# Node rows split into two parts of 12 bits in place of three of 8 for the gathering products of a graph kernel

## What is computed

```python
src, dst = (edge_index[0], edge_index[1])
for i in range(L):                      # L = 3
    msg = jax.nn.relu(x[src] + edge_attr)
    aggr = jax.ops.segment_sum(msg, dst, num_segments=N_NODES)
    h = x + aggr
    h = h @ W1[i] + b1[i]
    h = jax.nn.relu(_bn(h, g_mlp[i], be_mlp[i]))
    h = h @ W2[i] + b2[i]
    h = _bn(h, g_out[i], be_out[i])
    if i != L - 1:
        h = jax.nn.relu(h)
    x = h
```

## Time and profile before

| | us |
|---|---|
| median of 3 runs | 4912.82 (4910.23 to 4918.35) |
| profiled execution | 4920.59 |
| its span, first to last instruction | 4918.9 |
| busy in the span: TensorE / VectorE / GpSimd / ScalarE | 4251.6 / 3977.6 / 3219.8 / 2696.7 |

### The profile page before, as it was taken

How to read it: one execution, slowest core, us unless ns; L and a number is a source line. 1 busy time by engine, 2 the same in 40 slices (tenths; PEclk the granted TensorE clock), 3 DMA queues, 4 the chain that set the end, 5 groups by cost and what they waited for, 6 DMA issues and landing times.

```text
span 4918.9 us, 143637 instructions
## 1 busy us (share of the span) xinstructions
PE 4251.6 (86%) x50439; PEld 4136.7 (84%) x50440; DVE 3977.6 (81%) x7711; ACT 2696.7 (55%) x6908; POOL 3219.8 (65%) x2584
## 2 busy tenths in 40 slices
PE   2556655489999999969999997999999979999998
PEld 2556555489999999969999996999999969999996
DVE  7788888167777777778888887988888878888887
ACT  3899999257777777753343334433433353333334
POOL 0088888327777777737777773677777637777773
PEclk7777777699999999989999998999999989999998
DMA  9955554757777778758888885788888848888884
GB/s 123 319 188 193 171 190 166 240 161 250 248 249 249 248 249 249 239 177 278 278 281 282 279 279 170 245 279 281 279 276 281 271 145 281 277 279 282 277 280 135
DMA packets 664981, 1183.55 MB, mean 241 GB/s; under 512 B 152090, under 2 KB 489836, under 8 KB 664828
## 3 DMA queue, kind: packets, MB, share of 16 engines
q1 hardware_dynamic: 440796, 833.33, 53.3%
q10 hardware_dynamic: 142848, 181.89, 12.2%
q0 software_dynamic: 81184, 166.43, 10.3%
HBM read 966.87 MB, written 214.44 MB: 240 GB/s over the span
## 4 chain that ended last, share of the span: by engine, by line
PE 78%; issue 9%; DVE 6%; SPq 2%; DMA 1%; DVEq 1%; ACTq 1%; ACT 1%; POOL 0%; POOLq 0%; PEld 0%; PEldq 0%
PE ps L1721 24%; PE ps L1707 15%; PE ps L1636 13%; PE ps L1623 10%; PE ps L1731 6%; PE ps L1585 3%; PE ps L1586 3%; PE ps L1575 3%; DVEq L1420 1%; PE ps L1775 1%; DVE src_turned L1400 1%; DVE dst_hot L1407 1%; ACTq L823 1%; DVE agg L1422 1%; DVE sums L1415 0%
## 5 line engine op out<-in xcount | busy, mean ns | idle before, releaser
L728 POOL DMA_INDIRECT unit_x<-gin_rows,unit_src x1449 | 1788.3, 1234 | 670.3 <-PE ps L1721 389.5
L680 POOL DMA_INDIRECT attr_by_slot<-abuf,ridx x1080 | 1372.6, 1271 | 539.7 <-issue 328.0
L1721 PE MATMUL ps<-dst_hot,sums 128*128 128x128 f32 x10584 | 1520.7, 284 | 79.2 <-DVE agg L1422 71.4
L937 ACT ACTIVATE sums<-sums 128x512 f32<-128x512 f32 x1512 | 823.6, 571 | 1285.5 <-DVE sums L1415 1263.4
L1721 PEld LDWEIGHTS ps<-dst_hot,sums 128*128 128x128 f32 x10584 | 1306.9, 193 | 98.0 <-DVE agg L1422 84.4
L1707 PE MATMUL ps<-x_parts,src_turned 128*128 128x128 bf16 x15876 | 1143.5, 220 | 36.3 <-POOL x_parts L714 32.0
L1707 PEld LDWEIGHTS ps<-x_parts,src_turned 128*128 128x128 bf16 x15876 | 1027.0, 99 | 55.5 <-issue 40.3
L1415 DVE TENSOR_TENSOR sums<-ps,sums 128x512 f32<-128x512 f32 x1512 | 895.9, 615 | 8.4 <-PE ps L1707 8.4
L1407 DVE TENSOR_TENSOR dst_hot<-iota_one,dl_slot 128x896 f32<-128x896 f32 x756 | 818.9, 1083 | 2.2 <-DVE agg L1460 2.2
L846 ACT ACTIVATE val<-ps,val 128x128 f32<-128x128 f32 x2597 | 718.0, 375 | 180.5 <-DVE val L1261 180.5
L1636 PE MATMUL ps<-val,src_hot 128*128 128x129 f32 x5194 | 697.7, 284 | 1.9 <-DVE sums L1201 1.2
(11 more groups left out here) (242 smaller groups left out, 4133.4 us busy)
## 6 DMA issues: line engine op xcount, KB each, us to landing
sums<-attr_by_slot SPq DMA_DIRECT2D x756, 448.0 KB, 3.6
src_turned<-rows_by_group SPq DMA_DIRECT2D x756, 224.0 KB
turned_hot<-rows_by_block ACTq DMA_DIRECT2D x392, 384.0 KB
attr_by_slot<-zeros SPq DMA_DIRECT2D x36, 3136.0 KB, 17.1
unit_attr<-in_edge_attr SPq DMA_DIRECT2D x204, 448.0 KB
abuf<-in_edge_attr SPq DMA_DIRECT2D x72, 960.0 KB
unit_x<-gin_rows,unit_src POOLq DMA_INDIRECT x1449
attr_by_slot<-abuf,ridx POOLq DMA_INDIRECT x1080
```

Of the source, the lines that this page charges most:

```text
L680: pool.indirect_dma_start(out=attr_table, out_offset=bass.IndirectOffsetOnAxis(ap=ridx[:, g, t0 + t:t0 + t + 1], axis=0), in_=abuf[:, k % ...
L728: pool.indirect_dma_start(out=unit_x[:, half_place(k), t, :], out_offset=None, in_=gin_rows[n], in_offset=bass.IndirectOffsetOnAxis(ap=uni ...
L937: act.activation(attr[:, first:first + tiles, :], attr[:, first:first + tiles, :], ACT.Relu).then_inc(s_msg, 1)
L1721: ins = pe.matmul(ps[:, 7, 0:WINDOW], attr[:, b, :], dst_hot[:, HOT[c], b % G_TILES, :], start=(b == 0), stop=(b == BLOCKS - 1))
```

## The change

- The three bf16 parts become two of type float32r, a four-byte form of which a part holds 12 bits: `x_high`, ScalarE's copy of the rows to that type, and `x_low`, VectorE's difference. `x_high` lies over `flat`.
- Each tile has two products in place of three, and the ones (`src_turned`) become float32r too, in four buffers by HOT; SyncE loads the lanes to `src_rows` (bf16), behind a wait for the turning in place of the gather. VectorE's turning waits for the gather that last read the buffer.
- The parts are made at the end of a layer: VectorE copies turned chunks to `x_stage` (seven stages), SyncE stores them from there, two in flight, ScalarE makes the high part behind its normalising, VectorE the low part one chunk later. GpSimd has no part in it. In the first layer the rows lie in `work` (the tile of the attributes), and SyncE's first loads wait until they are turned, split and stored.
- KEEP_AT goes from 0 to 2: a unit's window addition comes at h = 9 and h = 2. TURN_LEAD stays 3 by value.

```diff
--- before.py
+++ after.py
...
+STAGES = 7
 G_LEAD = 3
 FIRST = 4
-TURN_LEAD = 3
+TURN_LEAD = min(HOT_SINCE)
 ADD_AT = 3
 SUM_AT = 4
-KEEP_AT = 0
+KEEP_AT = 2
...
-LAST_LEFT = BY_UNIT + 1
+LAST_LEFT = BY_UNIT + KEEP_AT + 1
...
-        x_parts, end = placed("x_parts", [P, PARTS, BLOCKS, D], BF16, at)
+
+        x_high, end = placed("x_high", [P, BLOCKS, D], F32R, at - 4 * COLS)
+        x_low, end = placed("x_low", [P, BLOCKS, D], F32R, at)
         dst_hot, at = placed("dst_hot", [P, HOTS, G_TILES, P], F32, end)
-        src_turned, at = placed("src_turned", [P, BLOCKS * P], BF16, at)
+        src_rows, at = placed("src_rows", [P, BLOCKS * P], BF16, at)
+        src_turned, at = placed("src_turned", [P, HOTS, G_TILES * P], F32R, at)
+
+        x_stage, _ = placed("x_stage", [P, STAGES, CHUNK], F32, at)
...
+        gx, gy = (of_moments[:, k * D:(k + STEP) * D].rearrange("p (s d) -> p s d", d=D) for k in range(2))
+        ghot = of_stat[:, 0:STEP * P].rearrange("p (s d) -> p s d", d=P)
...
-        s_gin_row = sem("gin_rows_stored")
+        s_gin_row = [sem(f"gin_rows_stored{k}") for k in range(2)]
...
+        def rows_stored(n, c):
+
+            return 16 * (n * len(range(c % 2, CHUNKS, 2)) + c // 2 + 1)
+
+        def all_stored(eng, n):
+            for c in (CHUNKS - 2, CHUNKS - 1):
+                eng.wait_ge(s_gin_row[c % 2], rows_stored(n, c))
...
+            def store_rows(n, of, ready):
+
                 for c in range(CHUNKS):
                     ready(c)
-                    rows = to[c * CHUNK:min((c + 1) * CHUNK, NODES)]
-                    sp.dma_start(rows if c == CHUNKS - 1 else rows.rearrange("(b p) d -> p b d", p=P),
-                                 rows_of(flat, c)).then_inc(done, 16)
+                    if c >= 2:
+                        sp.wait_ge(s_gin_row[c % 2], rows_stored(n, c - 2))
+                    rows = gin_rows[n][c * CHUNK:min((c + 1) * CHUNK, NODES)]
+                    sp.dma_start(rows if c == CHUNKS - 1 else rows.rearrange("(b p) d -> p b d", p=P), of(c)).then_inc(s_gin_row[c % 2], 16)
...
-                sp.wait_ge(s_gath, G_HALVES * done + 2 * c + 2 - G_HALVES + G_HALVES)
-                sp.dma_start(src_turned[:, c * G_TILES * P:(c + 1) * G_TILES * P],
+                if not isinstance(g, int) or done > 0:
+                    sp.wait_ge(s_sturned, G_CHUNKS * done + c + 1 - G_CHUNKS)
+                sp.dma_start(src_rows[:, c * G_TILES * P:(c + 1) * G_TILES * P],
...
-            sp.wait_ge(s_var, 2)
+
+            sp.wait_ge(s_turned, TURNS["gin_in"] + CHUNKS)
+            sp.wait_ge(s_low, CHUNKS)
+            all_stored(sp, 0)
             load_group(0, 0)
...
+                if n > 0:
+
+                    sp.wait_ge(s_low, CHUNKS * (n + 1))
+                    all_stored(sp, n)
...
-                for c in range(G_CHUNKS):
-
-                    of = slice(c * G_TILES, (c + 1) * G_TILES)
-                    pool.wait_ge(s_part, 2 * (G_CHUNKS * n + c) + 2)
-                    pool.tensor_tensor(x_parts[:, 2, of, :], unit_x[:, c % 2, :, :], x_parts[:, 1, of, :], ALU.subtract).then_inc(s_last, 1)
-                pool.wait_ge(s_last, G_CHUNKS * (n + 1))
-                pool.wait_ge(s_gin_row, 16 * CHUNKS * (n + 1))
+                pool.wait_ge(s_low, CHUNKS * (n + 1))
+                all_stored(pool, n)
...
+                if n == 0:
+                    for c in range(CHUNKS):
+                        normed(act, c)
+                        of = slice(BY_CHUNK * c, min(BY_CHUNK * (c + 1), BLOCKS))
+                        act.activation(x_high[:, of, :], work.rearrange("p (b d) -> p b d", d=D)[:, of, :], ACT.Copy).then_inc(s_high, 1)
+                        keep_columns(c)
...
+                def high_part(c):
+
+                    act.wait_ge(s_copied, TURNS[f"gin_out{n}"] + c + 1)
+                    if c == CHUNKS - 1:
+                        act.activation(x_high[:, BLOCKS - 1, :], x_stage[:, c % STAGES, 0:D], ACT.Copy).then_inc(s_high, 1)
+                    else:
+                        act.activation(part_of(x_high, c), staged(c), ACT.Copy).then_inc(s_high, 1)
...
+                        if m == 1 and c >= 2 and n + 1 < LAYERS:
+                            high_part(c - 2)
...
+                def low_part(c):
+
+                    vec.wait_ge(s_high, c + 1)
+                    of = slice(BY_CHUNK * c, min(BY_CHUNK * (c + 1), BLOCKS))
+                    vec.tensor_tensor(x_low[:, of, :], work.rearrange("p (b d) -> p b d", d=D)[:, of, :], x_high[:, of, :], ALU.subtract).then_inc(s_low, 1)
...
                 def turn_sources(i, c):
-                    of = src_turned[:, c * G_TILES * P:(c + 1) * G_TILES * P]
                     vec.wait_ge(s_lo[c], 16 * (n * BUCKETS + i + 1 + A_TILES))
-                    vec.tensor_scalar(of, of, lane_one[:, 0:1], None, ALU.is_equal).then_inc(s_sturned, 1)
+
+                    vec.wait_ge(s_gath, halves_before + G_HALVES * i + 2 * c + 2 - 2 * HOT_SINCE[c] + G_HALVES)
+                    vec.tensor_scalar(src_turned[:, HOT[c], :], src_rows[:, c * G_TILES * P:(c + 1) * G_TILES * P], lane_one[:, 0:1], None,
+                                      ALU.is_equal).then_inc(s_sturned, 1)
...
-                rest(0)
+                if n == 0:
+                    for c in range(CHUNKS):
+                        low_part(c)
                 for c in range(TURN_LEAD):
                     turn_sources(0, c)
-                rest(1)
...
+                def low_of_staged(c):
+
+                    vec.wait_ge(s_high, CHUNKS * (n + 1) + c + 1)
+                    vec.wait_ge(s_copied, TURNS[f"gin_out{n}"] + c + 1)
+                    vec.tensor_tensor(part_of(x_low, c), staged(c), part_of(x_high, c), ALU.subtract).then_inc(s_low, 1)
...
+                        if c >= STAGES:
+                            vec.wait_ge(s_gin_row[(c - STAGES) % 2], rows_stored(n + 1, c - STAGES))
+                        if c == CHUNKS - 1:
+
+                            link(vec.memset(x_stage[96:P, c % STAGES, 0:D], 0.0))
+                        vec.tensor_copy(staged(c), of).then_inc(s_copied, 1)
+                        if c >= 1:
+                            low_of_staged(c - 1)
...
-                        pe.wait_ge(s_last, G_CHUNKS * n + h // 2 + 1)
+                        pe.wait_ge(s_low, CHUNKS * n + (first + tiles - 1) // BY_CHUNK + 1)
                     for k in range(tiles):
                         b = first + k
-                        for part in range(PARTS):
-                            ins = pe.matmul(ps[:, BANK[h], k * D:(k + 1) * D], src_turned[:, b * P:(b + 1) * P], x_parts[:, part, b, :],
-                                            start=(k == 0 and part == 0), stop=(k == tiles - 1 and part == PARTS - 1))
+                        hot = src_turned[:, HOT[h // 2], b % G_TILES * P:(b % G_TILES + 1) * P]
+                        pe.matmul(ps[:, BANK[h], k * D:(k + 1) * D], hot, x_high[:, b, :], start=(k == 0), stop=False)
+                        ins = pe.matmul(ps[:, BANK[h], k * D:(k + 1) * D], hot, x_low[:, b, :], start=False, stop=(k == tiles - 1))
...
-                pe.wait_ge(s_gin_row, 16 * CHUNKS * (n + 1))
...
```

85 lines of the change are left out of this document (31 added, 54 removed).

## The result

The changed kernel takes **5127 us** (median of four runs, 5121 to 5132) against 4915 of the kernel before: a ratio of 1.043, 95% interval 1.041 to 1.045. It is slower, where the forecast was 4768 us. The time lies inside the stated range, but on the side that the forecast held for the less likely. The profiled execution has a span of 5130.0 us, 211.1 more than before.

A forecast was written before the change was run, and what follows sets the result against it. TensorE's order of work bound a group at 23.81 us; VectorE would then set 22.5, saving 137 us over 105 groups, plus 8 at layer ends: 4768 us median. Range 4735 to 5190, the forecast case's own 4735 to 4830.

The forecast's parts named there:

- What bounds now: Graph layers' loop: TensorE's order of work sets a group's 23.81 us, with VectorE 2.8 us behind.
- The gathers, p = 58 ns: TensorE's gather products: each float32r product costs p = 58 ns, so 98 take 5.7 us a group, 2.6 less.
- The quarter of a float32 product: TensorE's gathers: a float32 product is four passes in 233 ns, float32r needs one, so 58 ns.
- the transposes' 143 ns load: Sign for a cheap float32r weight load on TensorE: float32 transposes load in 143 ns, between bf16's 98 and float32's 192.
- The rule that was weighed: Skill's rule against the change: fast weight load only where the type is not float32; a plain one takes about 107 ns.
- TensorE's total: TensorE per group after the change: gathers 5.7, sums 11.69, units 3.02, wait about 0.85, together 21.3 us.
- The first rival: Four-byte weight load sets p at 108 to 119 ns: group 25.8 to 26.9 us, 5115 to 5230 us; chance 0.30.
- VectorE: VectorE's source turning slows from 473 to 656 ns, seven adding 1.3 us: 22.3 us a group, the new bound.
- Later window sums: KEEP_AT from 0 to 2 removes VectorE's waits at unit window additions, 2.5 us a group, letting it run at busy time.
- GpSimd "fits into 22.5": GpSimd's queue in the layers: 17.2 us of work a group, which fits into the new 22.5 us.
- The fourth rival: TensorE and VectorE, each waiting for the other, lose their gains: group stays at 23.8 us, 4905 us; chance 0.05.
- Ends of layers: Layer ends: longer VectorE turning but faster first chunks, -4 us for each of two layers, -8 together, between -20 and +20.

The follow-up runs named there:

- e_two_few: Changed kernel with bf16 parts (third left out), ones read as two-byte halves, and GpSimd gathering only four of each unit's seven tiles: 4736 us, 0.963 of the kernel before.
- e_two_again: Changed kernel with two bf16 parts (third left out) and ones read as two-byte halves of VectorE's four-byte tile: 4887 us, 0.994 of the kernel before.

## Why the prediction was wrong

- **What bounds now.** Right. TensorE's order of work set the group at 23.81, and it sets it at 25.81. That the bound would pass to VectorE was wrong, by the next step.
- **The gathers, p = 58 ns: this step failed.** It measured 112 ns between starts inside a run of products (116 with the change of line), and 98 x (0.112 - 0.058) = 5.3 us a group turned a VectorE-bound 22.5 into a TensorE-bound 25.8. The quarter of a float32 product was right for the columns and wrong for the product, since the load does not shrink with the passes. The row that should have decided stood in the earlier trace rows: 14 records with 64 columns come 108 ns apart, and the sums' records with 128 columns 119. Halving the columns gave almost nothing, so the load was already the price of any four-byte record (one by one, the starts of both lie 112 ns apart). I named 108 as "set by the weight load" and then let the transposes' 143 ns load argue against it; float32r's load is 192.
- **The rule that was weighed.** The Trainium skill (TensorE: Matmul & The Clock Gate, Weight-path perf modes) gives the fast load where the type is not float32. If float32r counts as float32, the page's formula for a plain load gives an estimate of 107 ns, near the 112 here. The trace shows float32r's load at 192 ns against bf16's 98.
- **TensorE's total.** The first rival's 25.8 us and 5115 us came out, though its terms did not all: gathers 7 x 1.63 = 11.4 us (10.6 was said), sums 7 x (0.64 + 0.86) = 10.5 (11.7), units 3.0, the wait for the window 0.58 (0.53). That sums to 25.5 of the 25.81. The gathers were 0.8 too low and the sums 1.2 too high, so the close total is partly luck; the 119 ns that I took for a record of the sums held the change from bf16 to four bytes, and six cost 107 each where four-byte ones come ahead of them too.
- **VectorE.** 21.03 + 1.3 was forecast. The turning takes 703 ns in the mean, 0.68 undisturbed, for my 656 and 628: 0.3 us a group too little. With TensorE fast enough the group is 22.22 and VectorE full (e_two_few), so the term was good to 0.3 us. It was hidden in the real kernel.
- **Later window sums.** The waits go, as said; what that brings was overrated (0.6 us a group where VectorE is the bound, nothing in the real kernel, minus 0.2% in the kernel before).
- **GpSimd "fits into 22.5".** Failed, and with the clock that fell behind the waits would have cost 150 us (4887 against 4736) even with p = 58. The fourth rival, no gain since engines wait for each other, was near this in size, with another mechanism.
- **Ends of layers.** -8 forecast. Between a layer's last window addition and the next one's first lie 84.4 and 83.0 us, 83.3 in the repeated kernel before: nothing. The turning phase grew as said; VectorE's first copy and last low part, then the targets of the first three chunks:

```profile
3126.11 0.69 DVE L1570 COPY x_stage<-ps 128x512 f32<-128x512 f32 x1 [2.06 <-PE ps L1813]
...
3140.92 0.88 DVE L1555 TENSOR_TENSOR x_low<-x_stage,x_high 128x512 fp32r<-128x512 f32 x2
...
3143.51 1.08 DVE L1431 TENSOR_TENSOR dst_hot<-iota_one,dl_slot 128x896 f32<-128x896 f32 x1
...
3146.82 1.09 DVE L1431 TENSOR_TENSOR dst_hot<-iota_one,dl_slot 128x896 f32<-128x896 f32 x1
...
3149.81 1.08 DVE L1431 TENSOR_TENSOR dst_hot<-iota_one,dl_slot 128x896 f32<-128x896 f32 x1
```

  15.7 us from the first copy to the end of the last low part (16.5 said). The chunks then come 3.0 to 3.3 us apart where it was 4.07; with the gathers at 56 ns the gap is 80.3 and 77.6 us (e_two_few), so this step lost its gain to the same p.

## What to carry to other kernels

Price a product by the distance between starts, and ask whether the load or the columns set it: two rows with different column counts and the same weights tell. A type that saves passes saves nothing when the weights change with every product of 128 columns and their load is the longer half. For a queue of small gathers, count the time between them as work, and expect each to stretch with VectorE's load: an engine at 77 to 79% busy by the profile was the next bound here. And look at the granted clock of the long groups: a wait of 1.9 us could cost 4.8, since TensorE stood still in it and came back at half its clock.

## What the runs showed of the hardware that I had not expected

- Float32r weights of 128 columns load in 192 ns records and let products start 112 ns apart; 256 float32r columns pass in 120 ns (start to start).
- A compare from bfloat16 into float32r takes 0.68 us for 896 elements, into float16 0.46.
- GpSimd's gather of 128 rows takes 0.94 to 2.36 us by what VectorE does beside it (a few up to 3.06); with VectorE full its mean is 1.63 us (e_two_few).
- After 1.90 us without work TensorE ran at the 1.2 GHz level for most of 8 us (granted clock 0.58, e_two_again), and the group took 27.0 us in place of 22.2.
